# Taking 55 products of identity tiles out of the set-up of a two-layer block on one core

## The chip, the cores and the metric

The kernel runs on one core of a Trainium2 chip. The metric is the device time of one execution in microseconds (us), lower is better. A core has TensorE (PE, matrix products into the eight PSUM banks), VectorE (DVE), ScalarE (ACT) and GpSimd (POOL), each with its own instruction stream; SyncE (SP) issues the DMAs. They meet only by semaphores.

## The reference, cut to what matters

The input `x` is 4 batches of 1024 rows by 512 features, `cond` one row of 128 numbers per batch. Two layers follow each other:

```python
# layer 0
scale = cond @ norm_w.T + 1.0
h = x * (scale[:, None, :] * rsqrt(mean(x * x, -1) + 1e-6))
val, gate = split(h @ up_w.T, 2, axis=-1)            # up_w is 4096 x 512
h = val * gelu(gate)
y = act_quant(h) @ weight_quant(down_w).T            # to 127 steps a row; to -1, 0, 1
x = y + x
# layer 1
Wd_b = Wd + 0.1 * (cond @ Wdd.T + bdd)               # one 128 x 512 matrix per batch
Wu_b = Wu + 0.1 * (cond @ Wdu.T + bdu)               # one 512 x 128 matrix per batch
x = x + relu(x @ Wd_b.T + bd) @ Wu_b.T + bu
```

## The kernel before, in words

The 4096 rows are worked off in eight chunks of 512. For a chunk, TensorE makes 32 sets of 12 products of 128x512 (`up_products`, lines 1023 to 1025): each number of `x` and of `up_w` is split into a high and a low 16-bit half, and high by high, high by low and low by high are summed in one bank, for four blocks of the features. The gate half of a slot `j` goes to the bank `GATE`, the value half to `VAL`; ACT takes the gelu, DVE multiplies. The products of the quantised result with `down_w` follow one chunk later. In chunk 0 the weights are also turned: `turn_w` (line 1002) transposes 128x128 tiles of `up_w` into a bank, ACT writes the high half `w_hi` (line 538) and DVE the low half `w_lo` (line 709).

Everything is in program order on each engine, written out by hand; there is no scheduler. The change lies in TensorE's set-up, which ends where `chunks(run)` begins. In order, TensorE there

- turns `cond` (lines 1195 and 1197), `norm_w` (1202), and multiplies the two (1208);
- turns the column `absmax` of the largest scale (1213), from which one power of two is to be found;
- turns the first two 128-row tiles of `x`, eight 128x128 transposes (1218), then spreads the maximum to all partitions (1220), from which DVE makes the factor `sc_now` in four short steps (lines 933 to 939);
- turns the other two tiles of `x`, eight transposes (1226), then the first weight tile, four transposes (1002);
- begins the first products (`first_products`, lines 1032, 1035 and 1038). The first of them needs `x_hi` (ACT, line 511, which needs `sc_now` and the first bank of 1226) and `w_hi` (ACT, line 538, which needs the four transposes of 1002).

Between these steps stands `keep_busy(count, bank)`: `count` products of the 16-bit identity tile `identb` with itself, 128x128 by 128 columns, into a bank that nothing reads before it is written again. They wait for nothing but `identb`, made by POOL at the start (line 459), and no other engine waits for them. There are 8, 4, 6, 9, 4, 4, 4 and 16, together 55. A transpose of a 32-bit tile is a product with the identity tile `identf` as well.

Of the kernel before, what the change touches and what calls it, by code (L numbers as in the profile page):

```python
# [15 lines left out]
P = 128  # L16
# [9 lines left out]
def conditioned_block(nc, x, cond, norm_w, up_w, down_w, Wd, bd, Wu, bu, Wdd, bdd, Wdu, bdu, out):  # L26
# [24 lines left out]
    with ExitStack() as ctx:  # L51
        def sb(name, shape, dt):
            return ctx.enter_context(nc.sbuf_tensor(name, shape, dt))
# [27 lines left out]
        identb = sb("identb", [P, P], BF16)  # L81
# [52 lines left out]
        bank = [ctx.enter_context(nc.psum_tensor(f"bank{i}", [P, 512], F32)) for i in range(8)]  # L134
        GATE, VAL = [bank[0], bank[1]], [bank[2], bank[3]]
        Y, HY, TA, TB = bank[4:8]
# [133 lines left out]
        def chunks(run):  # L270
            for c in range(NCH):
                run(c, c % 2, (c + 1) // 2 if c + 1 < NCH else None)
# [714 lines left out]
        def _(pe):  # L987
            def turn_w(jj, halves=range(2)):
                for p in halves:
                    i, m = 1 - p, 2 * jj + p  # L990
                    if jj == 1:
                        pe.wait_ge(w1_scaled, p + 1)
                        pe.wait_ge(ta_freed, 1)
                        pe.wait_ge(setup_dve, 4)
                    else:
                        pe.wait_ge(w_scaled, m + 1 - 2 * (jj > 1))
                    if jj == 2:
                        pe.wait_ge(w_lo_done, p + 1)
                    if jj > 2:
                        pe.wait_ge(w_lo_done, m - 1)  # L1000
                    for k in range(KD):
                        mm = pe.transpose(w_bank(jj)[i][:, k * P:(k + 1) * P], upn(jj, i)[:, k * P:(k + 1) * P], identf[:, :])  # L1002
                    mm.then_inc(w_turned, 1)
# [180 lines left out]
                        down_products(c - 1, j - 9)  # L1184


            def keep_busy(count, bank=Y):
                for _ in range(count):
                    pe.matmul(bank[:, 0:P], identb[:, :], identb[:, :], start=True, stop=True)

            pe.wait_ge(ident_ready, 4)
            keep_busy(8)
            pe.wait_ge(cond_in, 16)
            pe.wait_ge(cond_spread, 1)
            pe.transpose(VAL[0][:, 0:NB], cond_rows[:, :], identf[0:NB, 0:NB]).then_inc(delta_mm, 1)
            for a in range(HB):
                mm = pe.transpose(VAL[0][:, NB * (a + 1):NB * (a + 2)], cond_rep[:, a * P:(a + 1) * P], identf[0:NB, 0:NB])
            mm.then_inc(cond_turned, 1)
            keep_busy(4)
            pe.wait_ge(small_in, 16)  # L1200
            for k in range(KD):
                mm = pe.transpose(GATE[0][:, k * P:(k + 1) * P], g[:, 0, k * P:(k + 1) * P], identf[:, :])
            mm.then_inc(setup_pe, 1)
            keep_busy(6)
            pe.wait_ge(setup_act, 1)
            pe.wait_ge(cond_copied, 2)
            for k in range(KD):
                mm = pe.matmul(GATE[1][:, k * NB:(k + 1) * NB], g[:, 1, k * P:(k + 1) * P], condT[:, :], start=True, stop=True)
            mm.then_inc(setup_pe, 1)
            keep_busy(9)  # L1210
            pe.wait_ge(setup_dve, 3)
            pe.wait_ge(consts_ready, 3)
            pe.matmul(VAL[1][0:1, 0:P], absmax[:, :], identf[:, :], start=True, stop=True).then_inc(max_turned, 1)
            keep_busy(4)
            for t in range(2):
                pe.wait_ge(x_scaled, t + 1)
                for k in range(KD):
                    pe.transpose(x_bank(k)[:, t * P:(t + 1) * P], xn[:, t, k * P:(k + 1) * P], identf[:, :])
            pe.wait_ge(max_found, 2)
            pe.matmul(VAL[1][:, P:P + 1], ones[0:1, :], max_diag[:, :], start=True, stop=True).then_inc(max_spread, 1)  # L1220
            keep_busy(4)
            pe.wait_ge(x_scaled, 3)
            pe.wait_ge(x2_scaled, 1)
            for k in range(KD):
                for t in (2, 3):
                    mm = pe.transpose(x_bank(k)[:, t * P:(t + 1) * P], xn[:, t, k * P:(k + 1) * P], identf[:, :])
                mm.then_inc(ta_full, 1)
            keep_busy(4)
            turn_w(0, (0,))
            pe.wait_ge(setup_dve, 4)  # L1230
            keep_busy(16, VAL[1])
            chunks(run)


# [100 lines left out]
```

## Time and profile before

| | us |
|---|---|
| median of 3 runs (lowest, highest) | 961.24 (960.72, 961.3) |
| profiled execution, its own time | 961.1 |
| its span, first to last instruction | 959.3 |
| TensorE busy | 944.5 (98%) |
| VectorE busy | 685.0 (71%) |
| ScalarE busy | 437.6 (46%) |
| first instruction of TensorE | 1.92 |
| first product of `first_products` | 14.79 |

The profile is that of one execution, and all starts are counted from the first instruction of the span. Its own time is 1.8 us longer than the span. TensorE's records overlap: a product that follows another starts before the end of the one before, so how long a row of products takes is read from the distance of the starts or from the chain of waits, and not from the mean of one.

### The profile page before, as it was taken

The numbers are of one execution on the slowest core, as the hardware profiler recorded it, in microseconds if no ns is written. First come the engines' busy times: TensorE is split into PE (matmuls) and PEld (weight loads), VectorE is DVE, ScalarE is ACT, GpSimd is POOL, SyncE is SP. The second block draws the span as 40 slices with busy tenths as digits, with TensorE's granted clock in tenths as the row PEclk, the third lists the DMA queues.
The fourth block names the chain that finished last, engine by engine and source line by source line (L and its number), as shares of the span: only waits on it lengthen the run. The fifth ranks groups of instructions, "written<-read, shape, count | busy, mean of one in ns | idle before, by whom it ended". The sixth has DMA issues, their size and how long they took to land.

```text
span 959.3 us, 13747 instructions
## 1 busy us (share of the span) xinstructions
PE 944.5 (98%) x5318; PEld 465.9 (49%) x5318; DVE 685.0 (71%) x1058; ACT 437.6 (46%) x806; POOL 53.4 (6%) x53
## 2 busy tenths in 40 slices
PE   9999999999999999999999999999999999999997
PEld 6554544444444444444444444444444444445585
DVE  6777888866977577866977677856877675356665
ACT  7877678312742157312742257312742256115343
POOL 1000000000000000000000000000000000000664
PEclk9999999999999999999999999999999999999999
DMA  8644463474437643574436633573346641320584
GB/s 287 214 130 138 164 200 109 145 192 111 147 112 180 170 132 99 146 197 110 142 114 189 159 132 99 152 199 114 128 121 188 153 151 42 94 78 22 188 295 176
DMA packets 103770, 141.95 MB, mean 148 GB/s; under 512 B 35732, under 2 KB 41368, under 8 KB 103192
## 3 DMA queue, kind: packets, MB, share of 16 engines
q1 hardware_dynamic: 103704, 141.06, 48.6%
q8 instruction: 42, 0.69, 0.3%
q14 instruction: 24, 0.20, 0.1%
HBM read 112.72 MB, written 20.97 MB: 139 GB/s over the span
## 4 chain that ended last, share of the span: by engine, by line
PE 92%; DVE 3%; ACT 2%; issue 1%; DMA 1%; SPq 0%; DVEq 0%; ACTq 0%
PE bank L1023 22%; PE bank L1024 21%; PE bank L1025 21%; PE bank L1123 10%; PE bank L1082 6%; PE bank L1133 1%; PE bank L1002 1%; PE bank L1259 1%; PE bank L1251 1%; PE bank L1290 1%; PE bank L1280 1%; PE bank L1282 1%; PE bank L1291 1%; PE bank L1281 1%; PE bank L1272 1%
## 5 line engine op out<-in xcount | busy, mean ns | idle before, releaser
L1023 PE MATMUL bank<-x_split,w_hi 128*128 128x512 f16 x1016 | 385.4, 379 | 0.0
L1024 PE MATMUL bank<-x_split,w_hi 128*128 128x512 f16 x1016 | 385.1, 379 | 0.0
L1025 PE MATMUL bank<-x_split,w_lo 128*128 128x512 f16 x1016 | 385.1, 379 | 0.0
L768 DVE STREAM_TRANSPOSE delta_reg<-delta_reg 128x512 f32<-128x512 f32 x256 | 260.8, 1109 | 13.3 <-PE bank L1082 13.0
L584 ACT ACTIVATE g<-h 128x512 f32<-128x512 f32 x128 | 80.7, 630 | 268.4 <-DVE h L861 268.4
L861 DVE SCALAR_TENSOR_TENSOR h<-bank,desc,g 128x512 f32<-128x512 f32 x128 | 94.5, 738 | 105.8 <-issue 78.2
L573 ACT ACTIVATE g<-bank,desc 128x512 f32<-128x512 f32 x128 | 87.6, 684 | 164.8 <-PE bank L1025 164.7
L1023 PEld LDWEIGHTS bank<-x_split,w_hi 128*128 128x128 f16 x1016 | 99.4, 98 | 124.1 <-issue 10.3
L1025 PEld LDWEIGHTS bank<-x_split,w_lo 128*128 128x128 f16 x1016 | 99.4, 98 | 119.9
L1024 PEld LDWEIGHTS bank<-x_split,w_hi 128*128 128x128 f16 x1016 | 99.4, 98 | 111.3
L1123 PE MATMUL bank<-wqT,qreg 128*128 128x512 fp8e4 x448 | 101.3, 379 | 0.0
L778 DVE TENSOR_TENSOR absrun<-absrun,g 128x512 f32<-128x512 f32 x120 | 82.5, 688 | 24.5 <-ACT g L584 23.7
L750 DVE TENSOR_TENSOR h<-h,s_bc 128x512 f32<-128x512 f32 x112 | 71.8, 682 | 1.7 <-ACT s_bc L557 1.7
L1123 PEld LDWEIGHTS bank<-wqT,qreg 128*128 128x128 bf16 x448 | 43.8, 98 | 52.9
L820 DVE SCALAR_TENSOR_TENSOR xr<-bank,fy,xr 128x512 f32<-128x512 f32 x30 | 22.4, 751 | 64.3 <-DMA xr<-in_x 28.6
L550 ACT ACTIVATE h<-h 128x512 f32<-128x512 f32 x112 | 64.6, 623 | 8.0 <-DVE h L750 8.0
L553 ACT ACTIVATE qreg<-h 128x512 bf16<-128x512 f32 x112 | 63.6, 617 | 0.0
L1082 PE MATMUL bank<-delta_reg,cond_diag 128*32 128x256 f32 x1024 | 61.9, 382 | 0.5 <-DVE delta_reg L768 0.5
L468 POOL TENSOR_TENSOR rstd<-ss,mhalf 128x4 f32<-128x4 f32 x7 | 9.7, 1381 | 681.1 <-DVE ss L714 681.1
L1082 PEld LDWEIGHTS bank<-delta_reg,cond_diag 128*32 128x32 f32 x1024 | 30.0, 109 | 30.6 <-issue 13.1
L709 DVE TENSOR_TENSOR w_lo<-bank,w_hi 128x512 f16<-128x512 f32 x32 | 20.6, 684 | 13.4 <-ACT w_hi L538 13.4
L493 POOL TENSOR_TENSOR out_own<-xn,bu_bc 128x512 f32<-128x512 f32 x8 | 10.1, 1293 | 194.4 <-DVE h L966 191.9
(173 smaller groups left out, 641.3 us busy)
## 6 DMA issues: line engine op xcount, KB each, us to landing
delta_reg<-in_L_cond_Wdd SPq DMA_DIRECT2D x64, 512.0 KB, 3.7
delta_reg<-in_L_cond_Wdu SPq DMA_DIRECT2D x64, 512.0 KB, 3.7
qreg<-in_L_cond_up_w SPq DMA_DIRECT2D x32, 256.0 KB, 4.4
xr<-in_x SPq DMA_DIRECT2D x30, 256.0 KB, 4.1
x_scratch<-xr SPq DMA_DIRECT2D x30, 256.0 KB, 4.7
xn<-in_x SPq DMA_DIRECT2D x7, 1024.0 KB, 6.3
h<-in_L_cond_down_w SPq DMA_DIRECT2D x4, 1024.0 KB, 7.2
qreg<-in_L_cond_down_w SPq DMA_DIRECT2D x16, 256.0 KB, 3.9
```

What stands on the lines that cost most here:

```text
L550: act.activation(h[:, k, :], h[:, k, :], ACT.Copy, bias=ROUND).then_inc(round_added, 1)
L573: act.activation(g[:, j % 2, :], GATE[j % 2][:, :], ACT.Gelu, scale=desc[:, 2 * j + 1:2 * j + 2]).then_inc(gelu_done, 1)
L584: act.activation(g[:, j % 2, :], h[:, j, :], ACT.Abs).then_inc(abs_done, 1)
L750: dve.tensor_tensor(h[:, k, :], h[:, k, :], s_bc[:, :], ALU.mult).then_inc(h_scaled, 1)
L768: last = dve.transpose(natT[:, t, kk, :, :].rearrange("p a (r e) -> p e a r", e=4), nat[:, u % NAT, kk, :])
L778: dve.tensor_tensor(absrun[:, :], absrun[:, :], g[:, j % 2, :], ALU.max).then_inc(max_done, 1)
L861: dve.scalar_tensor_tensor(h[:, j, :], VAL[j % 2][:, :], desc[:, 2 * j:2 * j + 1], g[:, j % 2, :], ALU.mult, ALU.mult).then_inc(h_done, 1)
L1023: pe.matmul(bank[:, :], w_hi[:, k, cols], xh[:, par, k, :], start=(k == 0), stop=False)
L1024: pe.matmul(bank[:, :], w_hi[:, k, cols], xl[:, par, k, :], start=False, stop=False)
L1025: mm = pe.matmul(bank[:, :], w_lo[:, k, cols], xh[:, par, k, :], start=False, stop=(k == KD - 1))
L1082: mm = pe.matmul(HY[32 * t:32 * t + 32, cols], cond_diag[:, a, :], natT[:, (4 * m + t) % NATT, :, a, :], start=(a == 0), stop=(a == HB - 1))
L1123: mm = pe.matmul(Y[:, :], q[:, f, t * P:(t + 1) * P], wqT[:, f, :], start=(f == 0), stop=(f == FT - 1))
```

## The change

All eight calls of `keep_busy` are taken out, and the function with them. No other instruction and no wait is changed; the waits that stood behind a call still stand in the same order. Lines of the code behind the change have lower numbers afterwards: 1195 becomes 1190, 1213 becomes 1205, 1218 becomes 1209, 1220 becomes 1211, 1226 becomes 1216.

```diff
-            def keep_busy(count, bank=Y):
-                for _ in range(count):
-                    pe.matmul(bank[:, 0:P], identb[:, :], identb[:, :], start=True, stop=True)
-
             pe.wait_ge(ident_ready, 4)
-            keep_busy(8)
             pe.wait_ge(cond_in, 16)
             pe.wait_ge(cond_spread, 1)
             pe.transpose(VAL[0][:, 0:NB], cond_rows[:, :], identf[0:NB, 0:NB]).then_inc(delta_mm, 1)
...
             mm.then_inc(cond_turned, 1)
-            keep_busy(4)
             pe.wait_ge(small_in, 16)
...
             mm.then_inc(setup_pe, 1)
-            keep_busy(6)
             pe.wait_ge(setup_act, 1)
             pe.wait_ge(cond_copied, 2)
...
             mm.then_inc(setup_pe, 1)
-            keep_busy(9)
             pe.wait_ge(setup_dve, 3)
             pe.wait_ge(consts_ready, 3)
             pe.matmul(VAL[1][0:1, 0:P], absmax[:, :], identf[:, :], start=True, stop=True).then_inc(max_turned, 1)
-            keep_busy(4)
             for t in range(2):
                 pe.wait_ge(x_scaled, t + 1)
                 for k in range(KD):
                     pe.transpose(x_bank(k)[:, t * P:(t + 1) * P], xn[:, t, k * P:(k + 1) * P], identf[:, :])
             pe.wait_ge(max_found, 2)
             pe.matmul(VAL[1][:, P:P + 1], ones[0:1, :], max_diag[:, :], start=True, stop=True).then_inc(max_spread, 1)
-            keep_busy(4)
             pe.wait_ge(x_scaled, 3)
             pe.wait_ge(x2_scaled, 1)
             for k in range(KD):
                 for t in (2, 3):
                     mm = pe.transpose(x_bank(k)[:, t * P:(t + 1) * P], xn[:, t, k * P:(k + 1) * P], identf[:, :])
                 mm.then_inc(ta_full, 1)
-            keep_busy(4)
             turn_w(0, (0,))
             pe.wait_ge(setup_dve, 4)
-            keep_busy(16, VAL[1])
             chunks(run)
```

On TensorE, the end of the set-up stands so in the program before, from the turned maximum to the first product (`xn` is the tile of `x`, `qreg` that of `up_w`):

```order
L1213 MATMUL bank<-identf,absmax 1x128
L1189 MATMUL bank<-identb 128x128 x4
L1218 MATMUL bank<-identf,xn 128x128 x8
L1220 MATMUL bank<-max_diag,ones 128x1
L1189 MATMUL bank<-identb 128x128 x4
L1226 MATMUL bank<-identf,xn 128x128 x8
L1189 MATMUL bank<-identb 128x128 x4
L1002 MATMUL bank<-identf,qreg 128x128 x4
L1189 MATMUL bank<-identb 128x128 x16
L1032 MATMUL bank<-x_split,w_hi 128x512
```

And so it stands in the changed program, the same stretch of the same engine:

```order
L1205 MATMUL bank<-identf,absmax 1x128
L1209 MATMUL bank<-identf,xn 128x128 x8
L1211 MATMUL bank<-max_diag,ones 128x1
L1216 MATMUL bank<-identf,xn 128x128 x8
L1002 MATMUL bank<-identf,qreg 128x128 x4
L1032 MATMUL bank<-x_split,w_hi 128x512
```

Of the 55 identity products, 28 stood in this stretch, in four groups, and 27 in four groups ahead of it; what is left follows in the same order, and the other engines' streams are the same as before.

## Rows read from the trace of the kernel before

**Rows 1.** The page: busy time, the chain's shares, the largest group of products.

```profile
PE 944.5 (98%) x5318; PEld 465.9 (49%) x5318; DVE 685.0 (71%) x1058; ACT 437.6 (46%) x806; POOL 53.4 (6%) x53
...
PE 92%; DVE 3%; ACT 2%; issue 1%; DMA 1%; SPq 0%; DVEq 0%; ACTq 0%
...
L1023 PE MATMUL bank<-x_split,w_hi 128*128 128x512 f16 x1016 | 385.4, 379 | 0.0
```

**Rows 2.** The chain of waits in order of time: start us, us, what.

```profile
8.92 0.59 PE bank L1213 x2
9.51 0.54 PE bank L1189 x4
10.05 1.74 PE bank L1218 x8
11.79 0.39 PE bank L1220 x2
12.18 0.33 PE bank L1189 x4
12.51 0.88 PE bank L1226 x8
13.39 0.22 PE bank L1189 x4
13.61 0.44 PE bank L1002 x4
14.05 0.89 PE bank L1189 x16
...
21.91 0.46 ACT w_hi L538
...
25.10 0.40 DVE qreg L698
```

**Rows 3.** Single lines' instructions: ns min/median/max, first and last start.

```profile
L1218 PE MATMUL bank<-identf,xn x8: 421/421/454, 9.8 to 11.4; 128*128 128x128 f32 x8
...
L1220 PE MATMUL bank<-max_diag,ones x2: 245/295/345, 11.7 to 11.9; 1*128 1x1 f32 x2
...
L1226 PE MATMUL bank<-identf,xn x8: 272/272/279, 12.3 to 13.1; 128*128 128x128 f32 x8
```

**Rows 4.** Busy time in stretches of the set-up and behind it.

```profile
core 0: us, PE busy (x) PEld busy (x) DVE busy (x) ACT busy (x) POOL busy (x), PEclk, DMA share, GB/s
1.92:3.67 1.75, 1.63 (x13) 1.38 (x14) 0.78 (x1) 0.30 (x2) 0.74 (x4) 1.00 0.70 207
3.67:7.70 4.03, 3.98 (x24) 3.50 (x24) 1.01 (x7) 1.93 (x5) 0.00 (x0) 1.00 0.91 278
7.70:9.84 2.14, 2.04 (x16) 1.30 (x17) 1.83 (x9) 1.01 (x3) 1.31 (x2) 1.00 1.03 388
9.84:12.10 2.26, 2.26 (x12) 1.92 (x10) 2.01 (x8) 2.23 (x7) 0.36 (x1) 1.00 1.09 434
...
14.80:24.90 10.10, 10.10 (x59) 5.70 (x56) 8.37 (x22) 9.17 (x21) 0.00 (x0) 1.00 0.92 283
```

**Rows 5.** The timeline: start us, us, engine line op, count, idle before.

```profile
9.28 0.88 DVE L923 TENSOR_SCALAR xn<-xn,rstd 128x512 f32<-128x512 f32 x2 [0.16 <-POOL rstd L478]
...
9.82 1.57 PEld L1218 LDWEIGHTS bank<-identf,xn 128*128 128x128 f32 x8
...
13.05 0.69 ACT L511 ACTIVATE x_split<-bank,sc_now 128x512 f16<-128x512 f32 x1
...
14.09 0.60 ACT L538 ACTIVATE w_hi<-bank 128x512 f16<-128x512 f32 x1 [0.36 <-PE bank L1002]
...
14.74 0.10 PEld L1032 LDWEIGHTS bank<-x_split,w_hi 128*128 128x128 f16 x1
```

**Rows 6.** Waits that a DMA ended, 9 us to the end: us, times, longest.

```profile
DVE xr L820 <- DMA xr<-in_x: 28.6, 6, 5.3
ACT xr L531 <- DMA qreg<-in_L_cond_up_w: 0.6, 1, 0.6
```

## Prediction

> **What bounds the kernel now.** I read the page first. TensorE is busy for 944.5 of 959.3 us, and 92% of the chain that ended last is TensorE's own work [rows 1]. So a delay of TensorE anywhere on that chain lengthens the kernel by as much, and the question is whether the removed products stand on the chain or beside it.
>
> Next comes the chain in order of time through the end of the set-up [rows 2]. From 9.51 us it runs without a break over TensorE: identity products (0.54), transposes of x (1.74), the spread maximum (0.39), identity products (0.33), transposes (0.88), identity products (0.22), transposes of the weights (0.44), identity products (0.89), first products. The reader is to see that identity products lie on the chain in four places, and that eight transposes cost 1.74 us in one place and 0.88 in the next.
>
> That second point is looked up in the rows of the single lines [rows 3]. The eight transposes of L1218 have the same shape as the eight of L1226, and take 421 ns each against 272; their distance from one to the next is 1.74 / 8 = 0.218 us against 0.88 / 8 = 0.11. The two products of L1220, between them, took 345 and 245 ns. So TensorE ran at its lower level (1.2 GHz) until 11.7 and at its upper one (2.4 GHz) from about 12 us on. The granted clock in the table of stretches reads 1.00 from the first stretch [rows 4] and does not show this; I trust the durations, which change by a factor of two. Before the rise TensorE had been at work for 10 us, 9.9 of the 10.2 us from 1.92 to 12.10 (1.63 + 3.98 + 2.04 + 2.26) [rows 4], 31 of the 55 identity products among it.
>
> **The change part by part.** The sum is made against the profiled execution, 961.1 us (959.3 of span and 1.8 around it), which is 0.14 below the median of the runs, 961.24.
>
> *The first 27 products (8, 4, 6, 9).* They end before the turned maximum, which waits for DVE, not for them: behind them TensorE stands until absmax comes, and that product starts at 8.92 us [rows 2]. Their direct cost is 0, covered by the waits for cond, norm_w, ACT's copy and DVE's maximum. With them gone nothing else is late.
>
> *The 4 ahead of L1218.* The chain gives them 0.54 us, but their removal gives less back: L1218 needs the first tile of x from DVE, whose two instructions run from 9.28 to 10.16, the first to 9.72, and L1218's first weights were loaded at 9.82 [rows 5]. Gain between 0 and 0.10 us; I take 0.05.
>
> *The 4 ahead of L1226.* They are 0.33 us on the chain [rows 2], and nothing else holds L1226. Gain 0.33.
>
> *The 4 ahead of L1002.* 0.22 us [rows 2], gain 0.22.
>
> *The 16 ahead of the first product.* The chain gives them 0.89 us, but the first product needs w_hi, which ACT writes from 14.09 to 14.69, and its weights are loaded at 14.74 [rows 5]. So the 16 fill a wait of 0.6 us for ACT and the latencies around it. Gain 0 to 0.05; I take 0.
>
> *The clock.* If the upper level came at 12 us as before, the gains of 0.05 + 0.33 + 0.22 would not all arrive: w_hi waits for ACT too, which is at x_hi until 13.05 + 0.69 = 13.74 [rows 5]. It can start 14.09 - 13.74 = 0.35 us earlier at most, or 0.45 with the largest gain at L1218. But the engine now reaches the same point with much less work behind it. Ahead of L1218 only the few small products and four transposes of L1202 are left of what filled 1.92 to 9.84. The dense work begins at 9.8. When the clock then rises no row of before shows. It is bounded from both sides by the one rise that there is: before, it came 2.1 us after the dense transposes began (9.8 to 11.9), with all the work ahead of them, and 10.0 us after TensorE's first instruction (1.92 to 11.9). Counted from 9.8 that gives 11.9 and 19.8 us. I take a rise around 15 us, some 5 us after dense work begins, nearer to the shorter of the two because L1218's own transposes were the densest thing ahead of the rise before.
>
> With that, L1226 and L1002 run at the lower level, at the distance of L1218's: 8 x 0.218 = 1.74 us in place of 0.88 (+0.86), and 4 x 0.218 = 0.87 in place of 0.44 (+0.43). Sum: -0.05 - 0.33 + 0.86 - 0.22 + 0.43 = +0.69 us. w_hi then starts near 14.8 and ends near 15.4, the first product starts near 15.5 in place of 14.79, and TensorE stands idle for about 0.7 us between the last transpose and it, where the 16 were. If the rise falls into that wait, nothing more is lost.
>
> *What it is worth at the end.* Behind 14.8 TensorE is busy 10.10 of 10.10 us [rows 4], and where it then waits (25.10) it is for DVE, in a chain that ACT's w_hi of 21.91 began, which waited for TensorE's transposes [rows 2]. So no slack takes the delay up. A DMA could, if a load set the pace by its own time: after 9 us ACT waits once for one, 0.6 us, and DVE for the residual's rows [rows 6], whose loads are issued behind stores that wait for products themselves and so shift with them. I cost that at 0. Of the 0.69 us all reaches the end: 961.1 + 0.7 = 961.8 us.
>
> **A rule weighed.** L1218's transposes and L1220 are nearly all that TensorE did in the last 2 us before its durations fell from 421 to 272 ns [rows 3]; of identity products there were four, 0.54 us. The Trainium skill ("TensorE: Matmul & The Clock Gate", Part 4: PE-mode transpose) says that transposes do not count as work for the clock gate and that the full clock does not engage for them. By that rule the transposes from 9.8 to 14.8 would buy nothing, and the rise would wait for the first products; this is the second rival. The trace leans against it: 27 identity products, all of them before 8.92 us, had raised nothing, and the stretch with eight 32-bit transposes did.
>
> **The rivals.**
>
> *The identity products did not matter for the clock.* L1218 and L1220 alone raise it, at about 12 us again. For it: they fill the last 2 us before the rise. Against it: the work ahead of them was nearly without a pause, and is gone. Time: -0.35 to -0.45, so 960.7 us.
>
> *The clock rises late (slower than before).* The place is first_products and the gate half behind it. The price: each us of TensorE's work there at the lower level costs 0.5 us, since the stretch from 14.8 to 24.9 has no idle time [rows 4]. With a rise at T, after 15.5, the delay is 0.7 + (T - 15.5) / 2. At T = 19.8, the long bound above, it is 0.7 + 2.15 = 2.85 us, 963.9 us. It decides (over 0.2%, 1.92 us) from T = 17.9 us on. If transposes buy nothing and the first products at 15.5 need between 2.1 and 10.0 us, T is 17.6 to 25.5, and the delay 1.75 to 5.7; at 4.5 us of them, T = 20, 2.95 us, 964.1. For it: the 0.7 us of idle time ahead of the first product, now open, and that 7.9 us of filled set-up ahead of L1218 had not raised the clock. Against it: from 9.8 to 14.8 TensorE has 1.74 + 0.39 + 1.74 + 0.87 = 4.74 us of work with hardly a gap, twice the dense stretch that preceded the rise before.
>
> *Something gets over 0.2% faster.* All identity products on the chain are 0.54 + 0.33 + 0.22 + 0.89 = 1.98 us [rows 2], and 0.35 to 0.45 of it can come back; over 1.92 us would need a cause that the profile does not show.
>
> **How the numbers follow.** A change of under 0.2% (1.92 us around 961.24, so 959.3 to 963.2) can't be told from none. Forecast, a rise between about 12.5 and 17.9 us, centred on 961.8: 0.58. Rise at 12 again, 960.7: 0.22. Rise after 17.9, from 963.2 up, mostly 963.2 to 964.5: 0.17. Faster by a cause not seen: 0.03. So faster 0.03, same 0.58 + 0.22 = 0.80, slower 0.17. The range starts below the second case by half the spread of the runs shown (0.3), at 960.4, and goes up to 963.4, into the late case: little over 1 in 10 lies above, a few in 100 below.
>
> **What would show it.** In the profile of the changed kernel the transposes of L1216 (1226 before) and the first four of L1002 should take 421 ns as L1209's do (272 would be the first rival), the first product should start near 15.5, TensorE should idle for 0.7 us ahead of it, and the records of 128x512 products should be 379 ns [rows 1] from there on; if the first ones are longer, it is the late rise, and half of the time that they take is the price. The turned maximum should stay at 8.9, since TensorE was not late there. From the first product on, all engines' starts should be shifted by one and the same amount. The prediction fails if that shift is not kept to the end, if the set-up ahead of 8.9 us becomes slower, or if the clock stays low for many us of products.

## The result and the profile after

| | before | after |
|---|---|---|
| median of 22 runs each, us | 961.26 | 962.41 |
| lowest and highest | 960.68, 962.59 | 960.86, 965.69 |
| profiled execution, its own time | 961.1 | 963.88 |
| its span | 959.3 | 962.1 |

The ratio (it follows the means; that of the medians is 1.0012) is 1.0016, with a 95% interval of 1.0009 to 1.0023: the kernel became slower by 0.1 to 0.2%. More telling than the median is the spread, 4.8 us where it was 1.9. 13 of the 22 times lie from 960.86 to 962.79 and 9 from 963.37 to 965.69, the profiled execution, 963.88, among them. Of the 116 runs of the kernel before, here and in the experiments, one lies above 963 us (963.73). The upper part is what came with the change. Whether the times form two groups they do not show by themselves: the gap of 0.58 us is hardly wider than one within the upper part (964.79 to 965.36).

The chain of waits of the changed kernel in order of time (start us, us, what; L1209, L1211 and L1216 are 1218, 1220 and 1226 of before) answers to [rows 2]:

```profile
9.55 0.40 DVE xn L923
9.95 0.04 issue
9.99 1.97 PE bank L1209 x8
11.96 0.51 PE bank L1211 x2
12.47 1.90 PE bank L1216 x8
14.38 0.85 PE bank L1002 x4
15.23 0.73 issue
15.96 0.59 PE bank L1032
16.55 0.85 PE bank L1002 x4
17.40 0.43 PE bank L1035
...
19.54 0.43 PE bank L1038
19.96 0.30 PE bank L1035
20.26 0.22 PE bank L1032
...
25.06 0.46 ACT w_hi L538
...
28.25 0.40 DVE qreg L698
```

Eight transposes now cost 1.90 us where 0.88 stood, TensorE stands for 0.73 us ahead of the first product, and then each 128x512 product takes 0.43 us instead of 0.22 until about 20.0 us. The clock rose to its upper level (2.4 GHz) 8 us later than before; this moment is called the rise from here on. ACT's w_hi, at 21.91 before, is at 25.06: 3.15 us late. The single lines say the same, to be set against [rows 3]:

```profile
L1209 PE MATMUL bank<-identf,xn x8: 421/421/475, 10.0 to 11.5; 128*128 128x128 f32 x8
...
L1211 PE MATMUL bank<-max_diag,ones x2: 347/358/368, 11.9 to 12.1; 1*128 1x1 f32 x2
...
L1216 PE MATMUL bank<-identf,xn x8: 421/421/476, 12.4 to 14.0; 128*128 128x128 f32 x8
...
L1032 PE MATMUL bank<-x_split,w_hi x8: 379/380/634, 16.0 to 21.6; 128*128 128x512 f16 x8
```

In the last line the longest duration is the one to look at: of the eight products of L1032 some took 634 ns, some 379. The delay then travels through the kernel. The next transposes that TensorE waits for start at 28.69 in place of 25.55 (+3.14), and the span ends 2.8 later. The 0.3 in between lies in one place, about 122 us, the waits of TensorE for DVE's running maximum (engine, line waited for: us in total, times, longest), of before and of after:

```profile
PE bank L1107 <- DVE absrun L778: 1.8, 2, 1.2
```

```profile
PE bank L1107 <- DVE absrun L778: 1.5, 2, 1.0
```

It is not the delay that shortens this wait. In the second repeat of the changed kernel (below), with a w_hi 3.43 us late, it is 1.8 as before, and the span is 3.3 longer; in the run with more products between the small ones, with w_hi at 21.91 as before, it is 1.5, and the span is 0.5 shorter. The wait is about 0.3 us longer or shorter from one execution to the next, whatever the set-up did.

### The profile page after: what moved, and what is told of

Same layout as the page of the kernel before. It is cut to its first block, busy times and chain, and to the rows that moved or that the text cites. A ratio compares the mean times of both kernels' runs of the same rounds, so it can differ in the third digit from the quotient of the medians.

```text
span 962.1 us, 13637 instructions
## 1 busy us (share of the span) xinstructions
PE 943.2 (98%) x5263; PEld 463.7 (48%) x5263; DVE 684.4 (71%) x1058; ACT 437.7 (45%) x806; POOL 53.3 (6%) x53
## 4 chain that ended last, share of the span: by engine, by line
PE 92%; DVE 3%; ACT 2%; issue 1%; DMA 1%; SPq 0%; DVEq 0%; ACTq 0%
PE bank L1023 22%; PE bank L1024 21%; PE bank L1025 21%; PE bank L1123 10%; PE bank L1082 6%; PE bank L1133 1%; PE bank L1002 1%; PE bank L1247 1%; PE bank L1239 1%; PE bank L1278 1%; PE bank L1268 1%; PE bank L1270 1%; PE bank L1279 1%; DMA xn<-in_x 1%; PE bank L1269 1%
## 5 line engine op out<-in xcount | busy, mean ns | idle before, releaser
L493 POOL TENSOR_TENSOR h<-h,bu_bc 128x512 f32<-128x512 f32 x16 | 20.2, 1297 | 12.3 <-PE bank L1260 12.3
```

## The experiments

All medians below are of 11 or 12 runs (those without an interval of 1), and each ratio is to runs of the kernel before on the same chip. The place of the rise is read from the durations of TensorE's records, to some 0.3 us, and in each experiment from one profiled execution. Unchanged lines are left out of the diffs, and the remarks behind # are not in the kernel. The expectations name their theories by letters: A, the work in the last few us ahead decides the rise; B, all the work since the start does.

### The same program again

The changed kernel was profiled twice more, and the kernel before once.

> The changed kernel once more, for its rise and not for its time. Theory F (the moment of the rise differs from one execution of the same program to the next): first products at the lower level for some other length than the 4.0 us of the first profile, and the span differs by half of that difference; 0 to 5 us at the lower level, 960.9 to 965.7 us. Rival (the rise is fixed by the program, the spread comes from DMA): the first products leave the lower level at 20.0 us again.

> The changed kernel a third time, as the run before it: theory F expects a third moment of the rise with the span following it at half a microsecond for each, its rival 20.0 us again.

> The kernel before once more, for the place of its rise. Theory F (the moment of the rise differs from one execution to the next in this kernel too, but only within the set-up): between 11 and 14.5 us, at another place than 11.9; first product from 14.8 to 15.5. Rival (the 55 products fix it): L1218 at 421 ns and L1226 at 272 again.

The first repeat took 961.8 us, with a span of 960.0. Its chain:

```profile
9.78 1.97 PE bank L1209 x8
11.75 0.51 PE bank L1211 x2
12.26 1.90 PE bank L1216 x8
14.16 0.85 PE bank L1002 x4
...
15.75 0.38 PE bank L1032
16.12 0.44 PE bank L1002 x4
```

The first product is already at the upper level, so the rise fell into the pause, between 15.0 and 15.7. Up to there the two executions of one program are alike, piece by piece. The second repeat took 964.38 us, with a span of 962.6:

```profile
14.62 0.85 PE bank L1002 x4
...
16.21 0.58 PE bank L1032
16.80 0.85 PE bank L1002 x4
...
19.78 0.43 PE bank L1038
20.21 0.33 PE bank L1035
20.54 0.21 PE bank L1032
```

Here the rise came at about 20.3. So the moment is not fixed by the program: three executions gave 15.5, 20.0 and 20.3, with spans of 960.0, 962.1 and 962.6. A late rise costs as much as the upper part of the 22 times lies above the lower; that each of the 9 had one is inferred from this, and seen in one of them. The kernel before, repeated (961.09 us, span 959.3), rose within L1218 at about 11.2, where the first profile had 11.9:

```profile
10.31 1.37 PE bank L1218 x8
11.68 0.31 PE bank L1220 x2
```

### Only the last 28

```diff
-            keep_busy(8)
...
-            keep_busy(4)
...
-            keep_busy(6)
...
-            keep_busy(9)
```

> Only the last 28 identity products stand (4 ahead of the transposes of the first x tiles, 4 ahead of those of the others, 4 ahead of the weight tile, 16 ahead of the first product); the first 27 are out. Theory A (what raises the clock is how closely TensorE works in the last few us before; the late products matter): the rise comes by about 15 us in nearly every run, the median is 961.3 to 961.8, the spread stays near that of before (under 2 us). Theory B (all work since the start counts, so the early 27 matter): as the changed kernel, 962.4 or more, with runs up to 965. Theory C (the loss has nothing to do with the clock, it is only the shifted order at the first product): 961.3.

Median 962.25 us, 961.17 to 962.63; ratio 1.0007, interval 0.9998 to 1.0015. In its profile the rise came within the second transposes, at about 14.3:

```profile
12.63 0.54 PE bank L1189 x4
13.17 1.50 PE bank L1222 x8
14.66 0.22 PE bank L1189 x4
```

Theory A foresaw the missing tail (no run over 962.63), and missed the median by 0.5. In this profile the late products kept the rise out of the first products, but by themselves did not bring it as early as the 55 did.

### Only the first 27

```diff
-            keep_busy(4)      # ahead of L1218
...
-            keep_busy(4)      # ahead of L1226
...
-            keep_busy(4)      # ahead of L1002
...
-            keep_busy(16, VAL[1])
```

> Only the first 27 identity products stand (8, 4, 6, 9, all ahead of the turned maximum); the last 28 are out. Theory A: the rise comes later than in the kernel before in many runs, since the stretch from 8.9 us holds only transposes; median 961.8 to 962.6, highest above 964. Theory B: the early 27 have done their work, the rise comes at 12 us or earlier, and the 0.35 to 0.45 us of products on the path come back: 960.8 to 960.9.

Median 961.99 us, but 960.49 to 964.63, two of 12 over 964; ratio 1.0008, interval 1.0000 to 1.0016. The profiled execution, 964.63, rose at about 20.6:

```profile
13.06 1.90 PE bank L1224 x8
14.96 0.85 PE bank L1002 x4
15.82 0.73 issue
16.55 0.58 PE bank L1032
```

Theory B falls: 27 products ahead of 8.9 us do not prevent a late rise. Whether they make it rarer (2 of 12 runs here, 9 of 22 without them) so few runs do not decide.

### Only the 16

```diff
-            keep_busy(8)
...
-            keep_busy(4)
...
-            keep_busy(6)
...
-            keep_busy(9)
...
-            keep_busy(4)
...
-            keep_busy(4)
...
-            keep_busy(4)
```

> Only the 16 identity products ahead of the first product stand. In the changed kernel TensorE idles there for 0.73 us, and before that it stood idle twice ahead of the transposes. Theory A with the open pause as the cause: no late rise beyond 16 us any more, median 961.8, highest under 963.5. Theory A with the thin stretch ahead of 9.9 us as the cause: close to the changed kernel, 962.2 to 962.5. Theory B: 962.4 as well.

Median 962.87 us, 961.65 to 964.16; ratio 1.0014, interval 1.0005 to 1.0022. No theory had it that high. The rise came at about 16.0, in the midst of the 16, and the 16 have a price of their own:

```profile
15.17 1.34 PE bank L1189 x16
16.52 0.22 PE bank L1032
```

Begun at the lower level and ended at the upper one, they take 1.34 us where the pause is 0.73: what was free before (0.89 us beside ACT) lies on the path for 0.6. The profiled execution (964.16) is no measure of the rise alone. ACT's w_hi came 1.57 us late (23.48), but the span ended 2.8 late; the other 1.2 came at 125 us, where ACT waits 1.0 us for a load of down_w, which it does in no other profile here. Whether the change has a part in that, one execution does not tell. The chain there:

```profile
119.79 5.32 DMA qreg<-in_L_cond_down_w
...
126.23 0.75 DVE xr L760 x2
```

### All 55, as transposes

```diff
-                    pe.matmul(bank[:, 0:P], identb[:, :], identb[:, :], start=True, stop=True)
+                    pe.transpose(bank[:, :].bitcast(BF16)[:, 0:P], identb[:, :], identb[:, :])
```

> The 55 identity products stand where they stood, but each is issued as a 16-bit transpose of the identity tile (TensorE's transpose form) in place of a product. If transposes do not count as work for the clock: close to the changed kernel or later still, 962.4 to 965, and 128x512 products at the lower level in the profile. If they count as products do: 961.2 to 961.4, as before.

Median 961.5 us, 960.73 to 962.51; ratio 1.0000, interval 0.9992 to 1.0009. The rise fell at the start of the second transposes, about 12.9:

```profile
L1226 PE MATMUL bank<-identf,xn x8: 272/273/421, 12.5 to 13.5; 128*128 128x128 f32 x8
```

As far as these times tell, for 16-bit tiles a transpose does for the clock what a product does. The rule of the Trainium skill that was weighed in the prediction, that transposes do not engage the full clock ("TensorE: Matmul & The Clock Gate", Part 4: PE-mode transpose), does not hold here: the rise comes at 12.9 us, ahead of every product but the small ones of the condition and the maximum. The first repeat of the changed kernel says the same of 32-bit tiles: nothing but transposes and those small products stood ahead of its rise at 15.5 us, though two other executions of it did not rise there.

### Without the two groups of 4 on the path

```diff
-            keep_busy(4)      # ahead of L1226
...
-            keep_busy(4)      # ahead of L1002
```

> Of the 55 identity products only the 4 ahead of L1226 and the 4 ahead of L1002 are out, the 8 that lie on TensorE's path with nothing else to wait for; 27 + 4 + 16 stand. Theory A (the late products fill the stretch that decides the rise, even on the path): the rise is later in part of the runs, and the 0.35 to 0.45 us saved is lost again; median 961.5 to 962. Rival D (the 4 ahead of the first transposes and the 16 are enough): the rise stays at 12 to 14 us and the products on the path come back: 960.9 to 961.1.

Median 961.27 us, 960.37 to 962.23; ratio 1.0001, interval 0.9992 to 1.0010. Neither gain nor loss. The profile shows the exchange: the 8 are gone, but the transposes ran at the lower level to about 14.0, and w_hi was 0.49 later (22.40 against 21.91).

```profile
12.21 1.90 PE bank L1225 x8
14.11 0.44 PE bank L1002 x4
```

### Without all three groups of 4

```diff
-            keep_busy(4)      # ahead of L1218
...
-            keep_busy(4)      # ahead of L1226
...
-            keep_busy(4)      # ahead of L1002
```

> The three groups of 4 that lie on TensorE's path are out; 27 ahead of the turned maximum and the 16 ahead of the first product stand (43). Theory A (late filling decides whether the rise is over before the first products; the 16 stand where the changed kernel has its pause): no run above 963.5, median 961.3 to 961.8, between the kernel before and the one with the last 28 alone. Rival (the 4 ahead of the first transposes are what kept the rise early when the other 8 were taken out): runs up to 964 or more, median 962.

Median 961.96 us, 961.3 to 963.28; ratio 1.0008, interval 0.9999 to 1.0017; rise in the profile at about 15.1. The tail is short, as theory A had it (no run above 963.28), the median is that of the rival. The 4 ahead of the first transposes seem to be worth more than the other 8, but the intervals of this run and the one before it overlap.

### More between the small products

```diff
                 mm = pe.matmul(GATE[1][:, k * NB:(k + 1) * NB], g[:, 1, k * P:(k + 1) * P], condT[:, :], start=True, stop=True)
+                if k < KD - 1:
+                    keep_busy(2)
             mm.then_inc(setup_pe, 1)
-            keep_busy(9)
+            keep_busy(5)
```

> As the kernel before, but two identity products stand between each pair of the four condition products (L1208, 4 columns each), where TensorE is busy in the records without streaming much, and the 9 behind become 5 (57 in all). Theory E (the rise misses its first chance in the kernel before because the stretch of L1208 streams almost nothing): the clock rises before the transposes of L1218, which then take 0.88 in place of 1.74 us; up to 0.86 us faster in some runs, median 960.6 to 961.2. Rival (the rise is decided behind 9 us anyway): 961.4, or 0.1 to 0.3 more because L1208 gets longer.

Median 961.28 us, 960.44 to 962.39; ratio 1.0001, interval 0.9992 to 1.0009. The rise in the profile came at about 11.3, 0.6 earlier than in the first profile of before, and w_hi of turn 2 started at 21.91 as it had. The chain shows what holds it:

```profile
4.08 5.73 DMA qreg<-in_L_cond_up_w
9.84 0.73 ACT xr L531 x2
...
15.54 1.99 DVE x_split L720 x3
17.58 0.39 PE bank L1035
```

With an early rise the path leaves TensorE: it goes from the first load of up_w over ACT's squares to DVE's low halves. That is a floor of this set-up, as far as the load of up_w lands when it does here. The kernel before stands close to it: both run this product (the second of L1035) at 17.6. What theory E foresaw, a rise ahead of the transposes, did not come in this profile, and the median of 961.28 is nearer to its rival's 961.4; one profile does not exclude it. A repeat of the kernel before, without the products in between, rose at 11.2 too.

### 9, 4 and 16, and 9 and 4 alone

```diff
-            keep_busy(8)
...
-            keep_busy(4)
...
-            keep_busy(6)
...
-            keep_busy(4)      # ahead of L1226
...
-            keep_busy(4)      # ahead of L1002
...
-            keep_busy(16, VAL[1])      # in the second of the two alone
```

> 29 identity products: 9 ahead of the turned maximum, 4 behind it, 16 ahead of the first product. If the filling of the last few us ahead of the transposes is what counts, these 9 + 4 are worth as much as the 31: median 961.3, spread as before. If work further back counts too: 961.8 to 962.3, like the kernel with the last 28 alone.

> 13 identity products: 9 ahead of the turned maximum, 4 behind it; the pause ahead of the first product is open. If these 13 bring the rise to 11 to 14 us in every run, the open pause behind it does no harm: median 961.3, highest under 963. If the rise sometimes misses that stretch, the pause and the transposes ahead of it carry too little work and it comes only among the first products: some runs at 964 and over, as in the changed kernel and in the one with the first 27.

With 29 products: median 961.41 us, 960.6 to 962.8; ratio 1.0000, interval 0.9991 to 1.0009. They do what the 55 do. In its profile the rise came at about 11.5 and the first product at 14.30. With 13: median 961.36 us, 960.49 to 964.42; ratio 1.0004, interval 0.9996 to 1.0013. 11 of its 12 runs lie up to 963.09, one at 964.42, where the kernel before, on the same chip, had one of 17 at 963.73. In its profile (960.49 us) the rise came at about 12, and TensorE's path was short (its timeline: start us, us, engine line op, count, idle before):

```profile
9.89 1.95 PE L1215 MATMUL bank<-identf,xn 128*128 128x128 f32 x8
11.77 0.44 PE L1217 MATMUL bank<-max_diag,ones 1*128 1x1 f32 x2
12.14 1.09 PE L1222 MATMUL bank<-identf,xn 128*128 128x128 f32 x8
13.07 0.60 PE L1002 MATMUL bank<-identf,qreg 128*128 128x128 f32 x4
14.40 0.38 PE L1032 MATMUL bank<-x_split,w_hi 128*128 128x512 f16 x1 [0.73 <-ACT w_hi L538]
```

The first product starts at 14.40 where it had been 14.79. With 29 products and with 13, then, the two groups of 4 on the path do come back, 0.49 and 0.39 us at the first product. With 13, 0.22 of it are left at w_hi of turn 2 (21.69), since TensorE then waits for DVE's low halves, as it did with more products between the small ones. Whether the one run at 964.42 is a late rise, which no profile with the 16 showed, the times alone do not say.

No kernel beat the one before.

All profiles side by side. The third column is the first start of the transposes of the first two x tiles (L1218, or its line in that kernel), all in us:

| identity products that stand | run | transposes start | rise | highest of its runs |
|---|---|---|---|---|
| all 55 | before | 9.84 | 11.9 | 962.59 |
| all 55 | r_before | 10.10 | 11.2 | one run |
| 55, as transposes | e4_turned | 9.72 | 12.9 | 962.51 |
| 57, six of them between L1208's | e6_between | 9.89 | 11.3 | 962.39 |
| 8, 4, 6, 9; 4; 16 | e5_without_4_4 | 9.78 | 14.0 | 962.23 |
| 9; 4; 16 | e8_nine_four_16 | 9.87 | 11.5 | 962.80 |
| 9; 4 | e9_nine_four | 9.89 | 12.0 | 964.42 |
| 4, 4, 4, 16 | e1_last28 | 10.15 | 14.3 | 962.63 |
| 8, 4, 6, 9; 16 | e7_off_path | 9.96 | 15.1 | 963.28 |
| 16 | e3_only16 | 9.94 | 16.0 | 964.16 |
| 8, 4, 6, 9 | e2_first27 | 10.58 | 20.6 | 964.63 |
| none | after | 9.99 | 20.0 | 965.69 |
| none | r_after | 9.78 | 15.5 | one run |
| none | r_after2 | 10.24 | 20.3 | one run |

## Why the prediction was right or wrong

The forecast was no change, 961.8 us, from 960.4 to 963.4; measured were 962.41 and 0.16% (0.09 to 0.23). The time lies in the range, and the mechanism is the one named: a later rise, paid for on TensorE's path. Its sizes and chances were off, and that the first repeat took 961.8 us, the forecast to the tenth, is luck: an error and a scatter, each of about 0.3 us, cancel in it, as the terms on the set-up and on the slack show.

*First 27: 0.* Right in the direct sense. The turned maximum starts at 9.05 us against 8.92, behind a DMA of x that landed 0.13 later; in the repeats it starts at 8.88 and 8.80. What they are worth for the rise was put at nothing beside the direct cost, and seems to be more: the last 28 alone gave 962.25, against 961.43 with all 55 on the same chip, and their profile has the rise at 14.3 and w_hi 1.28 late; but the interval of that ratio (0.9998 to 1.0015) holds 1.

*4 ahead of L1218: -0.05.* In the profile L1209 began at 9.99, 0.15 late, with x itself; in the repeat at 9.78. Its end there, 11.75 against 11.79, makes -0.04, as good as the -0.05 put down.

*The set-up up to the first product, at the lower level of the clock: +0.69 in all.* The first repeat is the forecast case, a rise near 15. Its parts: -0.04 at L1209; +0.12 at L1211 (0.51 for 0.39), a term that I had left out, since in the kernel before the clock rose within that pair; +0.69 for the transposes (1.90 for 0.33 + 0.88), where I had 0.53, having priced them at the distance of a row of eight alone, 1.74; +0.19 for the weight tile, where I had 0.21. The sum is 0.96, and the first product was 0.96 late (15.75 against 14.79). The term was mis-sized by 0.27. The pause of 0.7 was 0.73.

*0.5 us for each us at the lower level.* Right. From the first product at 15.96 to the rise at 20.0 are 4.04 us, so 2.02; with the 1.17 by which that product was late, 3.19. Measured 3.15 at w_hi. In the second repeat: 1.42 + (20.3 - 16.21) / 2 = 3.47, and w_hi at 25.34 is 3.43 late.

*The 16 fill a wait: 0.* Right at the upper level. Its cover goes with the clock: 0.6 us on the path where they begin at the lower one (the 16 alone).

*No slack takes the delay up.* Right. The span is 2.8 longer with w_hi 3.15 late, 3.3 with 3.43, and 0.7 with 0.96. The differences go with the wait for DVE's running maximum, 1.5 us in the first and the third and 1.8 in the second; it is 1.5 also where w_hi was not late (the products in between), so it is scatter, and not slack that the delay fills. In the first repeat this 0.3 hides that the set-up had been priced 0.27 too low.

*When the clock rises.* This was the step that failed in its weight. I took one rise near 15 us and gave the late one, beyond 17.9, a chance of 0.17. Both are cases of one program: two of its three profiles had the late rise, and 9 of its 22 times lie above 963.2, where the late case was to begin. The reason that I gave against it, 4.74 us of nearly unbroken transposes, twice what preceded the rise before, is refuted by the profile itself: these transposes ran from 9.99 to 15.23, 5.2 us without a gap, and the clock stayed down through them and for 4 us of products and one pause of 0.73. With the first 27 in front it was the same (10.58 to 15.8). The first profile of before had suggested more: there four identity products and L1218 preceded the rise. With both the 9 ahead of the turned maximum (in one run 5, and six just before them) and the 4 behind it, all seven profiles rose from 11.2 to 14.0; with the 4 but not the 9 the one profile rose at 14.3, with the 9 but not the 4 the two rose at 15.1 and 20.6. The runs suggest that 32-bit transposes do less for the rise than 16-bit products that take as long. That is not shown: the identity products are of 16 bits and also fill the idle time of TensorE ahead of the transposes (1.20 and 0.36 us in the changed kernel), and no run parts the two. A run with 16-bit transposes of x alone in their place was not made.

*The rival that the identity products did not matter for the clock (0.22)* is refuted: no profile of the changed kernel (three) rose before 15 us, while the seven with the 9 and the 4 rose from 11.2 to 14.0. Its price was a little high, too: where the rise did come at 12 with the products on the path gone (9 and 4 alone), the first product came 0.39 earlier, inside the 0.35 to 0.45 forecast, but w_hi only 0.22.

What stays open: why the same program rises at 15.5 in one execution and at 20.3 in the next. Up to the pause the two chains are alike but for 0.46 us in the arrival of x. That may be more than chance: in the six profiles without the 4 ahead of L1218, the transposes that started at 9.78, 9.94 and 9.96 were followed by a rise from 15.1 to 16.0, those that started at 9.99, 10.24 and 10.58 by one from 20.0 to 20.6. But two of the first three also had the 16 in the pause, the border is 0.03 us wide, and no run moved the arrival of x alone; so this is a rival that stands untested.

## What to carry to other kernels

Work that fills TensorE's waits can be worth more than it costs even on the path, and the spread of many runs shows it before the median does: one profile of the changed kernel would have told 0.7 or 3.3 us. What matters is where it stands: 9 and 4 products just ahead of the critical transposes, with 16 behind them, did what 55 did; without the 16 the median was the same, but one run of 12 lay at 964.42. 27 products that all stood ahead of the turned maximum did not do it. Price such filling at both levels of the clock; what hides in a wait at 2.4 GHz (0.89 us) can stick out of it when it begins at 1.2 (1.34 us).

## What the runs showed of the hardware

- The rise to the upper level came at 15.5, 20.0 and 20.3 us in three executions of one program, and at 11.9 and 11.2 in two of the kernel before.
- 5.2 us of back-to-back 32-bit transposes (421 ns each in the records) were followed by the rise within 0.7 us in one execution and only 4.8 us later in two others; 16-bit transposes in the pauses did what 16-bit products do (ratio 1.0000).
- Each us that TensorE's products ran at the lower level cost 0.5 us: 4.04 us of them and a first product 1.17 late gave 3.15 at w_hi (3.19 by the sum).
- The granted clock in the tables of stretches read 1.00 from 9.8 to 14.9 and from 15.7 to 20.0 us in the changed kernel too, while products took 634 ns instead of 379 (a row of each):

```profile
9.80:14.90 5.10, 4.91 (x22) 4.49 (x22) 4.31 (x18) 4.03 (x10) 0.70 (x1) 1.00 1.03 414
...
15.70:20.00 4.30, 4.04 (x12) 2.07 (x13) 3.54 (x7) 4.27 (x10) 0.00 (x0) 1.00 0.71 192
```

At the start of a kernel the durations have to be read, not that column.
